# Deformable convolution beside a selective scan: ScalarE takes one of VectorE's three taps and weighs at the start of its unit

## The reference

```python
off_y, off_x, mask = conv(x_norm)                 # for each pixel and each of the 9 taps
samp = corner(y0i, x0i, wy0 * wx0) + corner(y0i, x0i + 1, wy0 * wx1) \
     + corner(y0i + 1, x0i, wy1 * wx0) + corner(y0i + 1, x0i + 1, wy1 * wx1)
samp = samp * mask[:, None]
return jnp.einsum('bcnhw,ocn->bohw', samp, wk)
```

```python
dA = jnp.exp(dt_l[..., None] * A)
h = dA * h + (dt_l * x_l)[..., None] * b_l[:, :, None, :]
y = jnp.einsum('bkdn,bkn->bkd', h, c_l)
```

## Time and profile before

| | |
|---|---|
| median of 3 runs | 15748.07 us (15738.32 to 15755.31) |
| the profiled execution's own time | 15757.44 us |
| its span, first to last instruction | 15755.4 us |
| mean granted TensorE clock | 0.789 |
| busy: PE, DVE, ACT, POOL | 12249.3, 11117.5, 9633.9, 5707.3 us |

### The profile page before, as it was taken

How to read it: one execution, slowest core, us unless ns; L and a number is a source line. 1 busy time by engine, 2 the same in 40 slices (tenths; PEclk the granted TensorE clock), 3 DMA queues, 4 the chain that set the end, 5 groups by cost and what they waited for, 6 DMA issues and landing times.

```text
span 15755.4 us, 180094 instructions
## 1 busy us (share of the span) xinstructions
PE 12249.3 (78%) x47232; PEld 7550.1 (48%) x47232; DVE 11117.5 (71%) x12583; ACT 9633.9 (61%) x20979; POOL 5707.3 (36%) x4760
## 2 busy tenths in 40 slices
PE   5777878788787878878778787887878778787745
PEld 4454554545545354453545545454453545536312
DVE  3486785858758586784858858587684867858586
ACT  1275674756657476674756747576574756747533
POOL 6452341514425153350524415144250523516100
PEclk8878778787787878879788787877879788797867
DMA  5442342423334232342423324233342423424100
GB/s 162 117 132 76 115 118 74 130 86 105 105 88 130 75 117 84 108 126 65 131 79 113 112 80 131 88 103 98 97 129 67 124 82 111 124 67 131 62 1 13
DMA packets 669382, 1559.15 MB, mean 99 GB/s; under 512 B 77720, under 2 KB 350300, under 8 KB 659516
## 3 DMA queue, kind: packets, MB, share of 16 engines
q0 software_dynamic: 368640, 1208.25, 26.1%
q1 hardware_dynamic: 289980, 298.08, 6.4%
q10 hardware_dynamic: 9216, 33.56, 0.5%
HBM read 1333.44 MB, written 206.14 MB: 98 GB/s over the span
## 4 chain that ended last, share of the span: by engine, by line
PE 40%; DVE 24%; DVEq 15%; issue 10%; ACT 7%; POOL 2%; ACTq 1%; DMA 1%; SPq 0%; POOLq 0%
PE psum L1144 6%; DVEq L906 6%; PE psum L1078 5%; DVE arena L910 4%; PE psum L1276 4%; PE psum L1088 4%; PE psum L1267 3%; DVEq L898 3%; PE psum L1097 2%; DVE arena L915 2%; DVE arena L881 2%; DVE arena L877 2%; DVE arena L879 2%; DVE arena L932 2%; PE psum L1048 2%
## 5 line engine op out<-in xcount | busy, mean ns | idle before, releaser
L645 POOL DMA_INDIRECT gathered<-cell_table,index x2880 | 3245.8, 1127 | 2990.3 <-PE psum L1078 1978.3
L645 POOL DMA_INDIRECT arena<-cell_table,index x1440 | 1969.0, 1367 | 2057.5 <-PE psum L1078 1760.9
L428 ACT COPY samples_t<-psum 128x384 f32<-128x384 f32 x1536 | 716.9, 467 | 2203.2 <-PE psum L1078 1957.8
L1088 PE MATMUL psum<-samples_t,pack 128*128 128x128 f32 x9216 | 1850.5, 384 | 273.3 <-ACT samples_t L428 273.3
L1177 PE MATMUL psum<-arena,pack 32*128 32x512 f32 x1024 | 834.9, 907 | 1468.8 <-DVEq L929 1468.8
L1088 PEld LDWEIGHTS psum<-samples_t,pack 128*128 128x128 f32 x9216 | 1725.1, 289 | 464.7 <-ACT samples_t L428 464.7
L1078 PE MATMUL psum<-pack,gathered 128*128 128x128 f32 x11520 | 1572.6, 295 | 439.5 <-DVE gathered L819 297.7
L1078 PEld LDWEIGHTS psum<-pack,arena 128*128 128x128 f32 x6912 | 1324.8, 216 | 1063.6 <-issue 1063.3
L1078 PE MATMUL psum<-pack,arena 128*128 128x128 f32 x6912 | 1537.1, 408 | 370.8 <-DVE arena L1004 243.7
L441 ACT ACTIVATE arena<-arena,weight 128x128 f32<-128x128 f32 x5760 | 1734.6, 390 | 7.4 <-DMA arena<-cell_table,index 7.4
L441 ACT ACTIVATE gathered<-gathered,weight 128x128 f32<-128x128 f32 x5760 | 1730.0, 389 | 0.7 <-DMA gathered<-cell_table,index 0.7
(11 more groups left out here) (164 smaller groups left out, 19704.5 us busy)
## 6 DMA issues: line engine op xcount, KB each, us to landing
cell_table<-arena SPq DMA_DIRECT2D x64, 2112.5 KB
gathered<-cell_table,index POOLq DMA_INDIRECT x2880, 3.8
arena<-in_x SPq DMA_DIRECT2D x16, 2048.0 KB, 7.7
image<-in_x SPq DMA_DIRECT2D x16, 2048.0 KB, 7.7
x_dram<-image SPq DMA_DIRECT2D x16, 2048.0 KB, 10.2
arena<-x_dram SPq DMA_DIRECT2D x16, 2048.0 KB, 7.9
out<-arena ACTq DMA_DIRECT2D x64, 512.0 KB, 3.9
arena<-cell_table,index POOLq DMA_INDIRECT x1440
```

Source lines behind the costliest of these rows:

```text
L645: pool.indirect_dma_start(gathered[m][:, n * CORNERS * C:(n + 1) * CORNERS * C], None, table, bass.IndirectOffsetOnAxis(ap=index[:, at:at ...
L1088: last = pe.matmul(psum[:, V_BANK, 0:TILE], wt("wconv")[:, n * C:(n + 1) * C], samples_t[:, n, :], start=n == 0, stop=n == TAPS - 1)
```

## The change

Group 0's third tap (four corners) goes from VectorE's instruction to four instructions on ScalarE, and ScalarE weighs that tap and group 1 at the start of its unit, ahead of the decays. The evacuation of (t-1, 2), which was the first step of ScalarE's unit, stands behind the decays. The order of the turns on PE is the same; the turn of group 0 waits for both engines. POOL's instructions are the same.

```diff
-BY_ACT = (1, 2)
+BY_ACT = (0, 1, 2)
+TAPS_V = 2
...
-                for at in range(GT * CORNERS):
+                for at in range(0 if m else TAPS_V * CORNERS, GT * CORNERS):
                     corner = gathered[m][:, at * C:(at + 1) * C]
...
-                    if with_next and not is_(t, 0):
-                        evacuate(b + 1, t - 1, 1 - par, 2)
+                    if with_next:
+                        weigh(b + 1, t, 0)
+                        weigh(b + 1, t, 1)
...
                     for j in range(2):
                         decays(0, slice(0, 1), j)
-                    if with_next:
-                        weigh(b + 1, t, 1)
+                    if with_next and not is_(t, 0):
+                        evacuate(b + 1, t - 1, 1 - par, 2)
                     if after:
                         soft(b, *after, 1 - par)
...
-                v.tensor_mul(corners, corners, w4.broadcast_to([128, GT * CORNERS, C])).then_inc(S["weighted_v"], 1)
+                v.tensor_mul(corners, corners, w4.broadcast_to([128, TAPS_V * CORNERS, C])).then_inc(S["weighted_v"], 1)
...
-                elif m in BY_ACT:
-                    pe.wait_ge(S["weighted_a"], ((a - 1) * TILES + t) * len(BY_ACT) + m - BY_ACT[0] + 1 + SEED["weighted_a"])
                 else:
-                    pe.wait_ge(S["weighted_v"], ((a - 1) * TILES + t) * (GROUPS - len(BY_ACT)) + m + 1)
+                    if m == 0:
+                        pe.wait_ge(S["weighted_v"], (a - 1) * TILES + t + 1)
+                        own_wait(pe)
+                    pe.wait_ge(S["weighted_a"], ((a - 1) * TILES + t) * GROUPS + m + 1 + SEED["weighted_a"])
```

More of the change, by code:

```diff
@@ L816, in weigh @@
                 own_wait(v)
-                corners = gathered[m].rearrange("p (n k) -> p n k", k=C)
-                w4 = weight4[:, bass.ds(t * TAPS + m * GT, GT), :].rearrange("p n (c o) -> p (n c) o", o=1)
-                v.tensor_mul(corners, corners, w4.broadcast_to([128, GT * CORNERS, C])).then_inc(S["weighted_v"], 1)
+                corners = gathered[m][:, 0:TAPS_V * CORNERS * C].rearrange("p (n k) -> p n k", k=C)
+                w4 = weight4[:, t * TAPS + m * GT:t * TAPS + m * GT + TAPS_V, :].rearrange("p n (c o) -> p (n c) o", o=1)
+                v.tensor_mul(corners, corners, w4.broadcast_to([128, TAPS_V * CORNERS, C])).then_inc(S["weighted_v"], 1)
             def add_tile(a, t):
```

## The result

The changed kernel takes 18,079.53 us (median of 4 runs, 18,068.1 to 18,087.72) against 15,751.69 us before (4 runs): a ratio of 1.148, interval 1.1466 to 1.1493. It is slower by about 2,330 us. The forecast was 18,728 us, the range 17,300 to 19,250.

The account below looks back on a forecast made before the run. VectorE was taken as the bound before; after, a ring through group 1's gather: 17.55 + 6.7 and 18.60 + 6.7, mean 24.78 us against 18.37, over 465 steps 2,980 us more, so 18,728 us, range 17,300 to 19,250.

Parts of the forecast that it names:

- The removal: L819 on VectorE, 1536 to 1024 elements: 0.53 us less in each of 480 units, buying nothing unless VectorE stayed the bound.
- the ring: Once per tile: turn (t, 0), six POOL issues, landing, group 1 weighing, decays, evacuation, convolution, next turn; mean 24.78 us.
- ScalarE's added work: Four weighings on ScalarE, 0.30 us each, 1.2 us a unit, held by its idle time.
- ScalarE's idle 3.09 us hold them: ScalarE's wait for the turn, ahead of evacuating (t-1, 2), was claimed to hold the added 1.2 us a unit.
- 0.79: Time in us from the end of the turn of group 0 to POOL's first issue.
- I choose 6.7 for the two: Convolution plus turn on PE, in us: 7.00 at clock 0.50, 3.79 at full clock; rise expected near the turn's end.
- the landing: Sixth POOL issue to data: 4.1 us from the trace, low 3.8, high 4.19; the skill's formula gave 2.6.
- the row: The trace's 4.1 us from sixth issue to data, preferred to the skill's 2.6 us, which would give 18,030 us.
- 31 steps an image: Rounds counted over 15 images: 465 steps at 6.41 us more each, 2,980 us in all.
- What is hidden: VectorE has nearly 5 us to spare before the decays, so its 0.53 us buys nothing.
- the flag: Flag matmul on PE behind two slow turns; named as what would be late next if VectorE's cover were gone.
- the signs named: Profile after: L885 steps 24 to 25.5 us, group 1's weighing waits 3 to 5, convolution 4.2, L826 idles 3 to 6.
- The direct wait: Rival: only decays, evacuation and convolution delay VectorE's L826; mean 20.1 us a step, 16,550 us; 10 in 100.

Follow-up runs that it names:

- the order alone: Kernel before, VectorE still weighing all of group 0; ScalarE's unit reordered to group 1, decays, evacuation of (t-1, 2): 18,090.47 us, ratio 1.1487.

## Why the prediction was right, and where its sizes were off

**The removal, 255 us, buys nothing here.** Right. L821 takes 1.226 us against 1.759 in the earlier trace rows, and VectorE waits 2,710 us at its L828 where it had 129.6. The same 255 us are worth some 200 (15,750 to 15,548 us) once the ring is open.

**ScalarE's added work is not the loss.** Right: the order alone costs the same as the whole change. That "ScalarE's idle 3.09 us hold them" is true only of work that stands ahead of the evacuation. Behind it the same four weighings made the kernel 172 us slower than before.

**The ring.** Right, shown from four sides: it opens when the evacuation goes first or group 1 goes out of it, it shrinks by one issue when one issue is left out, and by the clock when PE is kept busy. Terms for the 30 rounds of the image above, worked out from the starts in its timeline (mean, lowest to highest), against the prediction's:

| step | predicted us | measured us |
|---|---|---|
| start of convolution to first issue (convolution, turn, 0.79) | 7.49 | 6.64 (5.75 to 7.38) |
| first to sixth issue | 7.2 | 7.11 (6.26 to 8.19) |
| sixth issue to weighing | 4.1 | 3.97 (3.65 to 4.6) |
| twelve weighings | 3.60 | 3.52 |
| decays, mean of the orders | 1.86 | 1.75 |
| evacuation to convolution | 0.53 | 0.51 |
| ring | 24.78 | 23.51 |

The other images are no different: over all 450 rounds the ring is 23.52 us (21.75 to 25.24).

**The mis-sized term is PE's**: "I choose 6.7 for the two". Convolution and turn together took 5.85 us (6.64 less 0.79), 0.85 of the 1.27 us by which the ring was too long. The convolution was as predicted, 4.15 us in the mean of the 30 rounds against 4.21. The turn behind it took 1.70, where 6.7 leaves it 2.49. The stretches of the changed kernel show how (length, busy of PE first, PEclk third from the end), three of the round above and the turn of another:

```profile
7559.00:7564.50 5.50, 0.00 (x0) 0.00 (x0) 3.73 (x6) 4.66 (x14) 3.78 (x3) 0.80 0.34 96
7565.10:7569.30 4.20, 4.20 (x20) 4.20 (x21) 0.00 (x0) 4.05 (x6) 0.00 (x0) 0.52 0.15 49
7569.30:7572.00 2.70, 2.70 (x25) 2.53 (x24) 2.39 (x3) 1.69 (x6) 0.61 (x1) 1.00 0.01 3
...
7523.06:7525.27 2.21, 2.21 (x14) 2.21 (x14) 1.89 (x3) 0.39 (x1) 0.00 (x0) 0.61 0.00 0
```

PE rests 6.25 us, of which the first row shows 5.5, and the clock falls in it. PE does the convolution at 0.52 (4.20 us) and is at 1.00 when the turn begins, which then takes 1.32 us in the chain, not 2.79. In the last row the turn still has 0.61 and takes 2.21. The forecast that the rest costs the convolution its clock was right: all 450 convolutions began at the low level, behind rests of 4.5 to 10.4 us, and 20 of 450 did in the run with 24 added matmuls. The Trainium skill's rule that the prediction names ("TensorE: Matmul & The Clock Gate", section "HAM oscillation — how this bites in real kernels") fits this trace. That the turn too would be slow but for its end, as the earlier trace rows suggested with 5.5 us at 0.50, was mostly wrong: from its own start to its end it took 1.90 us in the mean and 2.57 at most, against 2.79. Six issues and the landing were sized well from the earlier trace rows.

The landing that the Trainium skill's formula gives ("DMA: Bandwidth & Descriptors", section "Anatomy of one DMA — SWDGE (gpsimd) path"), an estimate of 2.6 us, is in no round the stretch from the start of the sixth issue to the weighing, which is 3.55 us at least. Here the trace agrees with it if it is counted from the end of the issue: 7557.20 to 7559.84 in the rows below is 2.64 us, and the mean of the 450 rounds is 2.66. The ring has the issue's own 1.31 us in it as well, so the row was the right choice.

```profile
7555.89 1.31 POOL L647 DMA_INDIRECT gathered<-cell_table,index  x1 [0.31 <-issue]
...
7559.84 3.62 ACT L442 ACTIVATE gathered<-gathered,weight 128x128 f32<-128x128 f32 x12 [3.33 <-DMA gathered<-cell_table,index]
```

**The number of rounds was one too high.** I counted 31 steps an image. Unit 0 has no evacuation of a tile before it, so its step isn't a round: 17.56 us, less than the 19.44 of before (6505.24 to 6524.68). By the prediction's own ring that is 107 us over the 15 images, of the 649 by which the time was forecast too long; the ring's length accounts for 577. The rest nearly cancels: image 7 was a little quicker before than the mean of the images (27 us too much in the forecast), the stretches with the last tile, left out, grew by 45, and the profiled executions lie off the medians by 17 between them.

**What is hidden.** Right in kind: VectorE reached its part early and waited. In these rows the turn of group 2 and the flag did not come late. Of the signs named, two came out smaller: L887 steps by 23.5 us and not by 24 to 25.5, and group 1's first weighing waits 2.5 us a round for its gather, not 3 to 5, since ScalarE has already waited 3.7 us for the gather of the tap.

**The direct wait as a rival.** The run with group 1 taken out of the ring is that rival. It came at 16,181 us, not 16,550: its convolution was slow in a part of the tiles only (3.56 us in the mean; 1,788.8 us busy in all, below even the 1,850.5 of before), so the time lies between the 15.7 and 16.6 ms of its two clocks.

## What to carry to other kernels

Before a step goes ahead of another on an in-order engine, follow what the displaced step releases, engine by engine, until the path ends or comes back. If it comes back to the step that was moved forward, add up one round: that is the new least time of the loop, however little work was added. Put the added work where the engine waits already, ahead of the instruction that waits, not behind it: the same four instructions cost 170 us behind the evacuation and gave 200 ahead of it.

## What the runs showed of the hardware

PE's rests have a price that more work can lower. Twenty-four matmuls of no use a tile took 727 us off a kernel of 18,080, by keeping the granted clock up for the convolution behind them and the turn after it.

Where the low clock ends within a burst differs from round to round of the same work. In the round shown it was 1.00 right after the 4.2 us of the convolution, and in another of the same image it was still low for most of the turn (0.61 over 7523.06 to 7525.27). In the earlier trace rows it was 0.50 through all 5.5 us of a burst. So a duration taken from one burst behind a rest is one of a range, and here the mean turn (1.70 us) lay near the full-clock end of it.
